# Second cross attention of a two-layer perceiver: order of its front, last rows, first value tile and second context

## The reference, cut to what matters

```
x = x + xattn(_layernorm(x), ctx, ctx, mask, Wq, bq, Wk, bk, Wv, bv, Wo, bo)

q = _split_heads(query @ Wq + bq); k = _split_heads(key @ Wk + bk); v = _split_heads(value @ Wv + bv)
score = jnp.einsum('bhqd,bhkd->bhqk', q, k) / scale + mask * -1000000000.0
attn = jax.nn.softmax(score, axis=-1)
ctx = jnp.einsum('bhqk,bhkd->bhqd', attn, v)      # heads side by side again
return ctx @ Wo + bo
```

## Time and profile before

| | us |
|---|---|
| median of three runs | 1180.76 |
| the profiled execution | 1180.61 |
| its span, first to last instruction | 1179.3 |
| TensorE busy in the span | 1139.7 (97%) |
| VectorE busy | 744.1 (63%) |
| ScalarE busy | 527.0 (45%) |
| GpSimd busy | 242.0 (21%) |

### The profile page before, as it was taken

The page is one execution under the profiler, slowest core; times in us unless marked ns, Lnnn a source line. Parts: engine busy times, 40 slices in busy tenths (PEclk is TensorE's granted clock), DMA queues, the critical chain, the costliest instruction groups (busy, mean ns, idle before and its releaser), DMA issues.

```text
span 1179.3 us, 21706 instructions
## 1 busy us (share of the span) xinstructions
PE 1139.7 (97%) x8729; PEld 845.7 (72%) x8729; DVE 744.1 (63%) x1515; ACT 527.0 (45%) x1024; POOL 242.0 (21%) x296
## 2 busy tenths in 40 slices
PE   7999999999989999999999999999999999999997
PEld 4654477776547677777777777777887668887886
DVE  6467487749684656566566666665796866456632
ACT  3244445653122555555565656565553422223421
POOL 2300013266640152121212122221431100000000
PEclk9999999999999999999999999999999999999999
DMA  9769700100205155444444444454800402224211
GB/s 348 274 220 394 288 15 1 46 36 1 108 19 179 29 124 106 93 99 90 91 90 91 91 90 93 92 101 77 114 12 6 76 1 36 36 36 69 39 37 36
DMA packets 325671, 111.57 MB, mean 95 GB/s; under 512 B 301834, under 2 KB 302908, under 8 KB 321348
## 3 DMA queue, kind: packets, MB, share of 16 engines
q1 hardware_dynamic: 324224, 109.11, 36.6%
q10 hardware_dynamic: 1348, 1.09, 0.4%
HBM read 65.59 MB, written 20.97 MB: 73 GB/s over the span
## 4 chain that ended last, share of the span: by engine, by line
PE 89%; DVE 6%; ACT 2%; issue 1%; SPq 1%; DMA 1%; POOL 1%; DVEq 0%; ACTq 0%
PE bank L293 63%; PE bank L1867 3%; PE bank L1883 2%; PE bank L573 2%; PE bank L591 2%; PE bank L1161 2%; PE bank L1140 2%; PE bank L249 2%; PE bank L509 1%; PE bank L239 1%; SPq L324 1%; PE bank L1109 1%; PE bank L1093 1%; PE bank L1117 1%; PE bank L1106 1%
## 5 line engine op out<-in xcount | busy, mean ns | idle before, releaser
L1813 POOL COPY PT<-W 32x512 f32<-32x512 f32 x120 | 84.4, 703 | 311.6 <-DVE W L2008 230.4
L1997 DVE CUSTOM_DVE_ANT_0 W<-bank,W 128x512 f32<-128x512 f32 x128 | 80.8, 688 | 102.8 <-PE bank L1867 101.2
L2075 ACT ACTIVATE K<-bank,vecT 128x512 f32<-128x512 f32 x64 | 43.8, 690 | 167.5 <-PE bank L293 167.5
L2096 ACT ACTIVATE W<-W,low 128x512 f32<-128x512 f32 x128 | 90.7, 710 | 25.9 <-DVE low L1997 25.9
L293 PE MATMUL bank<-xT,wT 128*128 128x512 f32 x384 | 92.5, 390 | 0.8 <-ACT W L2973 0.5
L293 PE MATMUL bank<-Wkv,Wq 128*128 128x512 f32 x384 | 92.4, 395 | 0.0
L293 PE MATMUL bank<-Wkv,ctxT 128*128 128x512 f32 x384 | 92.1, 395 | 0.0
L293 PE MATMUL bank<-Wq,Wkv 128*128 128x512 f32 x384 | 90.0, 390 | 1.6 <-DVE Wq L310 1.6
L293 PE MATMUL bank<-ctxT,Wkv 128*128 128x512 f32 x384 | 89.8, 392 | 0.0
L293 PE MATMUL bank<-woT,hR 128*128 128x512 f32 x384 | 87.8, 390 | 0.7 <-DVE W_late L2894 0.5
L293 PEld LDWEIGHTS bank<-Wkv,ctxT 128*128 128x128 f32 x384 | 70.8, 188 | 22.5 <-ACT K L2075 5.7
(11 more groups left out here) (363 smaller groups left out, 2095.9 us busy)
## 6 DMA issues: line engine op xcount, KB each, us to landing
PT<-W SPq DMA_DIRECT2D x360, 64.0 KB, 2.1
W<-ctx_turned SPq DMA_DIRECT2D x16, 1024.0 KB, 5.8
W<-in_ctx_dram SPq DMA_DIRECT2D x8, 1024.0 KB, 11.2
ctx_turned<-ctxT SPq DMA_DIRECT2D x8, 1024.0 KB, 8.2
ctx_turned<-W SPq DMA_DIRECT2D x8, 1024.0 KB, 7.1
XT<-in_ctx_dram SPq DMA_DIRECT2D x4, 1024.0 KB, 12.2
XT<-in_L_ffn_wi_dram SPq DMA_DIRECT2D x64, 64.0 KB, 2.1
raw_own<-in_ctx_dram SPq DMA_DIRECT2D x3, 1024.0 KB, 11.7
```

Source lines behind the costliest of these rows:

```text
L1813: pool.tensor_copy(there, here).then_inc(kept_p.s, 1)
L1997: dve.tensor_tensor_reduce(out=PR[:, j, :], in0=bank[:, 4 + j % 4, :], in1=mask, scale=1.0, scalar=3.0e38, op0=ALU.add, op1=ALU.min, accum ...
L2075: act.activation(K[:, m, :], bank[:, n % 4, :], ACT.Identity, bias=pcol("L1_xattn_bk", m)).then_inc(ring_a.s, 1)
L2096: act.activation(PR[:, j, :], PR[:, j, :], ACT.Exp, bias=low[:, j:j + 1], scale=-1.0, accum_out=total[:, j:j + 1]).then_inc(expd.s, 1)
```

## The change

In the front, the last two row blocks are copied in four separate halves, part 1 of blocks 6 and 7 first, then part 0, with ScalarE waiting for VectorE's low half before it reads the same bank again. Three of key tile 3's twelve matmuls go behind the last transposes. The query products wait for part 1's low halves at the first tile and for part 0's at the third, and the eight query tiles start at bank 6 instead of bank 4. For image 0, value tile 0 is made ahead of the first scores and value tile 1 between the two score groups, and VectorE copies value tile 0 ahead of the first four transposes of probabilities. Context 1 is split ahead of the image loop: ScalarE's casts wait for the last query product and stand ahead of the table load, VectorE's low halves stand behind the mask's product. The loop is unchanged for the other images.

```diff
--- before.py
+++ after.py
@@ -1717,6 +1717,7 @@
             xn5 = XT[:].rearrange("p c n -> p (c n)").rearrange("p (g d) -> p g d", g=G)
             row5_banks = kept["row5_banks"]
             views = [split_parts(x_parts, g, 4 + g % 3) for g in range(G)]
+            last_parts = ((G - 2, 1), (G - 1, 1), (G - 2, 0), (G - 1, 0))
 
             ctx_at = (ctxT, Wq)
 
@@ -1849,6 +1850,15 @@
                 product(b, lambda h, c: Wkv[:, h, 0, c, m * P:(m + 1) * P],
                         lambda h, c: ctx_at[i % 2][:, h, c, :], C).then_inc(ring.s, 1)
 
+            def first_keys_pe(lo, hi):
+
+                if lo == 0:
+                    free_bank("key", 0, 3)
+                ins = product(bank[:, use_of["key", 0, 3] % 4, :], lambda h, c: Wkv[:, h, 0, lo + c, 3 * P:4 * P],
+                              lambda h, c: ctx_at[0][:, h, lo + c, :], hi - lo, first=(lo == 0), last=(hi == C))
+                if hi == C:
+                    ins.then_inc(ring.s, 1)
+
             def values_pe(i, k):
                 product(free_bank("value", i, k), lambda h, c: ctx_at[i % 2][:, h, c, k * P:(k + 1) * P],
                         lambda h, c: Wkv[:, h, 1, c, :], C).then_inc(ring.s, 1)
@@ -1907,26 +1917,32 @@
                     elif g == 2:
                         pe.wait_ge(xt_a.s, xt_a.base)
                     transpose_rows(xn, 3, g, 4 + g % 3)
-                    if g in (2, 5):
-                        keys_pe(0, 2 + g // 3)
-                pe.wait_ge(xt_v.s, xt_v(2 * G - 1))
+                    if g == 2:
+                        keys_pe(0, 2)
+                    elif g == 5:
+                        first_keys_pe(0, 3)
+                first_keys_pe(3, C)
                 pe.wait_ge(wt_v.s, wt_v.base)
                 u = 0
                 for n in (1, 0):
                     for m in range(C):
+                        if u in (0, 2):
+                            pe.wait_ge(xt_v.s, xt_v(2 * G - 3 + u))
                         if u >= 4:
                             pe.wait_ge(q_v.s, q_v(u - 4))
-                        product(bank[:, 4 + u % 4, :], lambda h, c: Wq[:, h, c, m * P:(m + 1) * P],
+                        product(bank[:, 4 + (u + 2) % 4, :], lambda h, c: Wq[:, h, c, m * P:(m + 1) * P],
                                 lambda h, c: x_parts[n][:, h, c, :], C).then_inc(proj.s, 1)
                         u += 1
                 for i in range(NI):
                     more = i < NI - 1
+                    if i == 0:
+                        values_pe(0, 0)
                     scores_pe(i, 0)
-                    values_pe(i, 0)
+                    values_pe(i, 0 if i else 1)
                     scores_pe(i, 1)
                     if i:
                         attend_pe(i - 1)
-                    values_pe(i, 1)
+                        values_pe(i, 1)
                     if not more:
                         last_probs_pe(0)
                     values_pe(i, 2)
@@ -2008,21 +2024,27 @@
                 dve.transpose(PR[:, j, :], PR[:, j, :]).then_inc(probs.s, 1)
 
             def vector():
-                for g in range(G):
+                for g in range(G - 2):
                     for k, (high, low_half, src) in enumerate(views[g]):
                         dve.wait_ge(xt_a.s, xt_a(2 * g + 1))
                         split_v(low_half, src, high).then_inc(xt_v.s, 1)
                     if g == 1:
                         normalise(xn, 3, G - 1)
+                for n, (g, k) in enumerate(last_parts):
+                    high, low_half, src = views[g][k]
+                    dve.wait_ge(xt_a.s, xt_a(2 * (G - 2) + n))
+                    split_v(low_half, src, high).then_inc(xt_v.s, 1)
                 u = 0
                 for n in (1, 0):
                     for m in range(C):
                         dve.wait_ge(proj.s, proj(u))
-                        dve.tensor_scalar(qT[:, m, n * 512:(n + 1) * 512], bank[:, 4 + u % 4, :], pcol("L1_xattn_bq", m),
+                        dve.tensor_scalar(qT[:, m, n * 512:(n + 1) * 512], bank[:, 4 + (u + 2) % 4, :], pcol("L1_xattn_bq", m),
                                           -scale, ALU.add, ALU.mult).then_inc(q_v.s, 1)
                         u += 1
                 dve.wait_ge(mask_in.s, mask_in(1))
                 v(dve.tensor_scalar(mask, mask, 1e9, None, ALU.mult))
+                for c in range(C):
+                    context_v(1, c)
                 for i in range(NI):
                     more = i < NI - 1
                     j = i // 2 - 1 if i and i % 2 == 0 else None
@@ -2031,19 +2053,23 @@
                     recips_v(i, 0)
                     for t in range(4, XPAIRS):
                         scores_v(i, t)
+                    if i == 0:
+                        value_v(0, 0)
                     if more:
                         for t in range(4):
                             probs_v(i, t)
                         recips_v(i, 1)
-                    value_v(i, 0)
+                    if i:
+                        value_v(i, 0)
                     if i:
                         attended_v(i - 1)
                     if not more:
                         value_weight_v((0, 1))
                     value_v(i, 1)
                     if more:
-                        for r in range(4):
-                            context_v(i + 1, r)
+                        if i:
+                            for r in range(4):
+                                context_v(i + 1, r)
                         for t in range(4, XPAIRS):
                             probs_v(i, t)
                     else:
@@ -2103,13 +2129,21 @@
 
             def scalar():
                 act.wait_ge(carried.s, carried(0))
-                for g in range(G):
+                for g in range(G - 2):
                     act.wait_ge(turned.s, turned(3 * G + g))
                     for high, low_half, src in views[g]:
                         act.copy(high, src).then_inc(xt_a.s, 1)
+                for n, (g, k) in enumerate(last_parts):
+                    act.wait_ge(turned.s, turned(3 * G + g))
+                    if n >= 2:
+                        act.wait_ge(xt_v.s, xt_v(2 * (G - 2) + n - 2))
+                    act.copy(views[g][k][0], views[g][k][2]).then_inc(xt_a.s, 1)
                 act.wait_ge(proj.s, proj(3))
                 for m in range(C):
                     key_a(0, m)
+                act.wait_ge(proj.s, proj(7))
+                for c in range(C):
+                    context_a(1, c)
                 for i in range(NI):
                     more = i < NI - 1
                     act.activation(carrier[:, 3:4], carrier[:, 2:3], ACT.Exp)
@@ -2118,7 +2152,7 @@
                     scaled_a(i, 0)
                     for j in range(4, XPAIRS):
                         scores_a(i, j)
-                    if more:
+                    if more and i:
                         for r in range(4):
                             context_a(i + 1, r)
                     scaled_a(i, 1)
```

## The result

The changed kernel took 1183.74 us (median of 12 runs, 1179.79 to 1184.65), the kernel before beside it 1180.53 us (12 runs, 1179.32 to 1182.49). The ratio is 1.0021, 95% interval 1.0012 to 1.0029: about 2.5 us slower (the medians alone stand 3.2 us apart; the ratio is used from here on). A second series of it, among the experiments, gave 1.0020 (1.0011 to 1.0029). The forecast of 1180.4 us was wrong, and so was its range; rival (b) is what happened.

What follows compares the result with a forecast made beforehand. TensorE was taken as the bound, with SyncE's serial queue next in line. Front gains of 1.58 + 1.01 + 1.6 = 4.2 us shrink to 0.35 at the attend: 1180.76 - 0.35 = 1180.4 us, range 1178.2 to 1182.9.

Steps and rivals of the forecast that it cites:

- rival (b): At image 0's attend, the new stall of about 3.85 us drops TensorE's clock: 1182.1, up to 1183.8 us; chance 0.18.
- Step 1: Last rows and split key tile: queries start at 368.34 instead of 369.92 us, gain 1.58, 0.40 us idle left.
- Step 2: Value tile 0 ahead of first scores: TensorE's gap closes, gain 1.01 us; scores start at 393.05 against 392.97.
- Step 3: Second context split early: image 1's keys lose their 1.73 us gap, gain 1.6; its first scores start at 414.9.
- Step 4: Image 0's attend: SyncE's probability queue lands at 423.8, TensorE waits from 420.0; all but 0.35 us is given back.
- (a): At image 0's attend, landing does not decide or queue drains sooner: 1176.6 us, half-way 1179.0; chance 0.18 for both.
- (c): Front gaps stay, as handshake or three late matmuls cost what they save: 1180.4 to 1181.3 us; chance 0.07.

Runs made afterwards that it cites:

- The shortened queues: Changed kernel with context 2's load issued behind image 0's second half of probability moves (0.9990 of the kernel before), or ahead of all of them (0.9990).
- the part that moved the cause as well: Kernel before with only the last row blocks in four halves and key tile 3 split: 1179.56 us, ratio 0.9984.
- copy behind: Changed kernel with VectorE's copy of value tile 0 back behind the first four probability transposes: 1181.55 us, 1.0002 of the kernel before.
- the kernel with the attend later: Changed kernel with the attend of image i-1 moved behind value tile 1, from image 1 on: 1180.88 us, 0.9993 of the kernel before.
- that with the load behind as well: Changed kernel with the attend behind value tile 1 and context 2's load behind image 0's second half of moves: 1178.57 us, 0.9979 of the kernel before.
- The fastest kernel: Changed kernel with context 2's load ahead, value tile 0's copy in VectorE's wait for exponentials, attend behind value tile 1: 1177.79 us, 0.9965 of the kernel before.

## Why the prediction was wrong, step by step

**Step 1** was right: the queries started at 369.07 less 0.6, 368.47, for 368.34 foreseen, with 0.32 us idle for 0.40. One reading in it does not add up: two casts of 0.39 us do not fit between 367.77 and 368.45, where the pair took 0.68; the error in the queries' start is 0.13 us.

**Step 2** was right: no gap before the first scores, and these at 393.78 less 0.6, 393.18, for 393.05.

**Step 3** was right in this kernel: no gap before the key tiles, image 1's scores at 414.75 for 414.9. What I did not see is that the early split holds up the softmax chain as soon as the first scores come sooner (1.25 us in the run without the value tile ahead).

**Step 4** was right in its mechanism and nearly in size. The first issue came at 404.55 less 0.6, 403.95, for 403.94; the stall was foreseen as 3.85 and was 4.38. The mis-sized terms: the queue took 17.98 us instead of 17.70, as its long issue took 2.36 us, and from the landing to the first matmul it is 0.24 us, for which I had allowed 0.09 (403.94 + 19.8 is 423.74, not 423.8). Together they took the 0.35 us of gain that were to be left. The shortened queues confirm that the end of the issues sets the landing: 2.4 us less of issuing, 2.4 us less of stall. Why one issue behind the context's load is held for 2.36 us is not shown; the load's own traffic may be the reason.

**The clock** is the step that failed. The sum of step 4 charged the new stall with its own length alone and put the clock's price at nothing; it was 2.5 us (2.51 in the profile; 0.22% by the run that kept TensorE at work). I had it among the rivals with 0.18, for two reasons. The stall was "little more than what passed there" before the only fall whose start the trace showed, and the gap of 1.75 us "shows nothing of it". Both came from one execution. The runs show a fall at stalls of 4.38 and 4.55 us, of 3.08, and of 1.98 and 1.96 us in profiles of other kernels; a stall of 1.36 and one of 1.50 us at the attend passed without one. In 22 of the changed kernel's 23 runs the mean clock was 0.994 to 0.996; in the three series of experiments it was 0.997 or more in 90 of 97 runs of the kernel before. In the one run with 0.997 the changed kernel took 1179.79 us, 2.6 us under its next. So the stall brings the clock down in nearly every execution, and where it seems not to, the loss is gone.

The rule that the rival was judged by was wrong too: "whether the clock falls before the landing ends the stall". In the kernels with stalls of 1.98 and 3.08 us the clock fell some 0.6 and 0.9 us after TensorE had gone back to work, and it cost 1.6 us all the same. So a stall that ends before the fall is not safe.

The price of 1.7 to 3.4 us was right, and so was the time of that rival, 1182.1 to 1183.8, though the lower price was taken from the first transposes after the start, and the profile gives a granted clock of 1.00 there (8 to 12 us): that they were slow by the clock is not shown. The Trainium skill ("TensorE: Matmul & The Clock Gate", section "🎯 Why this matters for your kernels") warns of idle gaps between bursts of matmuls. The falls in the stalls of 4.38 and 4.55 us agree with it, and I gave it too little weight against a single trace. The range ended at 1182.9 because I cut off the upper half of this rival.

Rivals (a) and (c) are out: the landing does decide the attend's start, and the gaps were closed.

What stays open: why one and the same stall brings the clock down in one profile and not in another, as the one near 930 us below does. Nothing here varied a stall's place in time by itself.

## What to carry to other kernels

Before an edit that moves the bottleneck engine's work ahead, follow the next transfer that it will ask for back to its first cause. If this cause does not move too, the gain turns into a wait; here 4.4 us of closed gaps became one of 4.4 us, while the part that moved the cause as well kept all of its gain. A wait gathered in one place can be dearer than the same time in small gaps, because TensorE's clock may fall in it or just behind it, and the matmuls behind it pay (1.6 to 2.5 us here). And look for idle time in the queue itself: the load that stood between the two halves could be issued 17 us earlier (395.4 instead of 412.7), once context 1 was split early, and no cost of this shows.

## What the runs showed that was not expected

TensorE's clock fell at stalls as short as 1.72 us, and a fall at the attend cost 1.6 us (copy behind) to 2.5 us (the changed kernel).

The kernel before has such a place too, in a stage that no kernel here changes. Near 930 us TensorE waits 1.72 or 1.73 us in all fourteen profiles. In nine of them the clock falls there, in five it does not. These are TensorE's timelines around it and a stretch, first of the kernel with the attend later, then of that with the load behind as well:

```profile
930.15 1.25 PE L239 MATMUL bank<-ident,W 128*128 128x128 f32 x8 [1.72 <-DVE xT L310]
...
930.00:935.00 5.00, 4.85 (x33) 3.42 (x34) 5.00 (x11) 3.37 (x7) 1.50 (x6) 1.00 0.79 123
...
928.30 1.31 PE L239 MATMUL bank<-ident,W 128*128 128x128 f32 x8 [1.73 <-DVE xT L310]
...
930.00:935.00 5.00, 5.00 (x25) 3.62 (x24) 3.85 (x9) 2.87 (x6) 0.00 (x0) 0.72 0.75 118
```

From the stall's end to the same later product it is 946.00 - 930.15 = 15.85 us in the first and 945.75 - 928.30 = 17.45 in the second: the fall costs 1.6 us. The fastest kernel's profile has it as well, that of the kernel before happened not to. So some of every kernel's spread, 2.2 to 5.9 us among the experiments, comes from this place, and one profile does not say whether a stall brings the clock down. The mean clock of each run says more: in the runs with the attend later it splits them into two groups about 2.5 us apart, though where the slower ones had their falls no profile shows.
